# Two of eight experts for every token, the other six only for their picked tokens

## What is computed

```python
h = tok(x, ...)          # 64 images: patches -> windows (attention over 9 positions) -> 4 patch tokens and a class token, 256 wide
h = concat([cls_tok, h], axis=1)                       # 6 tokens per image, 384 rows in all
h = h + attn(layernorm(h), Wq, Wk, Wv, Wp, bp)         # 16 heads, causal, 6 tokens
h = h + ffn(layernorm(h), gate_w, gate_up_w, down_w)
...
def ffn(x, gate_w, gate_up_w, down_w):                 # 8 experts, 256 -> 2*512 -> 256
    router_probs = softmax(x @ gate_w)
    top_k_probs, top_k_idx = top_k(router_probs, 2)
    top_k_probs = top_k_probs / sum(top_k_probs)
    hidden = silu(x @ gate) * (x @ up)                 # for each expert
    expert_out = hidden @ down
    return sum over the two picked experts of expert_out * its probability
```

## Time and profile before

| | us |
|---|---|
| median of 3 runs | 228.7 (227.08 to 228.98) |
| the profiled execution's time | 228.78 |
| its span, first to last instruction | 227.0 |
| router's logits finished, on the trace's clock | 129.62 |
| experts on PE, from then to the last matmul | 129.62 to 223.5 |

### The profile page before, as it was taken

The page is one execution under the profiler, slowest core; times in us unless marked ns, Lnnn a source line. Parts: engine busy times, 40 slices in busy tenths (PEclk is TensorE's granted clock), DMA queues, the critical chain, the costliest instruction groups (busy, mean ns, idle before and its releaser), DMA issues.

```text
span 227.0 us, 4002 instructions
## 1 busy us (share of the span) xinstructions
PE 207.6 (91%) x1368; PEld 192.4 (85%) x1368; DVE 155.6 (69%) x363; ACT 101.6 (45%) x225; POOL 79.5 (35%) x91
## 2 busy tenths in 40 slices
PE   2999989999999988789587989999999999999983
PEld 2898969898987878477386889999999999999983
DVE  2565981929696767577987599576957785858541
ACT  3754581835354516334122177383718371717030
POOL 0037093555428302270643315233423332333200
PEclk9999999999999999969889999999999999999999
DMA  6999910002910000000000005172533253400004
GB/s 222 360 394 373 339 52 3 3 0 54 423 80 1 3 0 0 0 3 0 1 0 0 3 0 206 76 277 53 225 128 149 43 234 97 180 0 3 0 0 69
DMA packets 4890, 23.01 MB, mean 101 GB/s; under 512 B 694, under 2 KB 2444, under 8 KB 3724
## 3 DMA queue, kind: packets, MB, share of 16 engines
q1 hardware_dynamic: 3960, 21.26, 26.3%
q10 hardware_dynamic: 916, 1.58, 2.0%
HBM read 22.44 MB, written 0.39 MB: 101 GB/s over the span
## 4 chain that ended last, share of the span: by engine, by line
PE 82%; DVE 8%; ACT 3%; DMA 2%; issue 2%; POOL 0%; SPq 0%; DVEq 0%
PE bank L744 26%; PE bank L757 15%; PE bank L419 11%; PE bank L496 9%; PE bank L539 4%; PE bank L434 3%; DMA raw<-conv_w 2%; PE bank L443 2%; PE bank L634 2%; PE bank L618 2%; PE bank L643 1%; PE bank L476 1%; DVE stats L1162 1%; PE bank L657 1%; PE bank L694 1%
## 5 line engine op out<-in xcount | busy, mean ns | idle before, releaser
L744 PE MATMUL bank<-split 128*128 128x322 f32 x384 | 59.2, 314 | 0.6 <-DVE vprod L1531 0.6
L744 PEld LDWEIGHTS bank<-split 128*128 128x128 f32 x384 | 57.6, 188 | 0.9 <-issue 0.9
L1147 POOL TENSOR_TENSOR split<-raw,split 128x256 fp32r<-128x256 f32 x32 | 29.0, 906 | 56.7 <-DVE split L1484 56.7
L757 PE MATMUL bank<-split 128*128 128x256 f32 x288 | 36.0, 283 | 0.6 <-DVE split L1537 0.6
L757 PEld LDWEIGHTS bank<-split 128*128 128x128 f32 x288 | 35.4, 192 | 0.8 <-DVE split L1537 0.8
L419 PE MATMUL bank<-split 128*128 128x256 f32 (+1 forms) x225 | 28.2, 284 | 1.0 <-DVE split L1259 1.0
L419 PEld LDWEIGHTS bank<-split 128*128 128x128 f32 (+1 forms) x225 | 27.5, 191 | 1.5 <-DVE split L1259 1.4
L1044 POOL TENSOR_TENSOR rstd<-veps,mhalf 128x1 f32<-128x1 f32 (+2 forms) x17 | 14.2, 838 | 38.5 <-DVE veps L1169 38.4
L496 PE MATMUL bank<-split 128*128 128x512 f32 x108 | 26.9, 399 | 0.0
L1011 ACT ACTIVATE vprod<-bank 128x322 f32<-128x322 f32 x32 | 13.9, 436 | 24.8 <-PE bank L744 24.7
L1531 DVE TENSOR_TENSOR vprod<-bank,vprod 128x322 f32<-128x322 f32 x32 | 15.7, 491 | 12.0 <-PE bank L744 8.5
(11 more groups left out here) (161 smaller groups left out, 276.2 us busy)
## 6 DMA issues: line engine op xcount, KB each, us to landing
raw<-ffn_w SPq DMA_DIRECT2D x8, 1536.0 KB, 6.5
raw<-xa SPq DMA_DIRECT2D x5, 768.0 KB
tok<-tok_w SPq DMA_DIRECT2D x1, 1536.0 KB, 12.4
tok<-tok_w SPq DMA_DIRECT2D x1, 776.0 KB, 6.4
raw<-xa ACTq DMA_DIRECT2D x1, 576.0 KB, 5.1
raw<-xb SPq DMA_DIRECT2D x6, 96.0 KB
att<-att_w SPq DMA_DIRECT2D x1, 488.0 KB, 13.9
raw<-conv_w SPq DMA_DIRECT2D x1, 384.0 KB, 5.7
```

Of the source, the lines that this page charges most:

```text
L744: mm = pe.matmul(bank[b][:, 0:NCOL], aws[:, q, pw, a:a + P], ms[:, px, c, FIRST:ROWS], start=(c == 0 and m == 0), stop=(c == CC - 1 and m ...
L757: mm = pe.matmul(bank[b][:, 0:C], hids[:, px, s * FQ + q, a:a + P], bws[:, s, pw, q * C:(q + 1) * C], start=(q == 0 and m == 0), stop=(q = ...
L1147: pool.tensor_tensor(bws[:, s, LO, q * C:(q + 1) * C], b_raw[:, s, q, :], bws[:, s, HI, q * C:(q + 1) * C].bitcast(F32), ALU.subtract).the ...
```

## The change

Experts 0 and 1 (DENSE = 2) still run over all tokens. For experts 2 to 7 each token's up to two picks are given a slot: slots are sorted by expert, each expert begins at a tile of 128 slots, and there are always SLOT_TILES = 10 tiles. DVE computes the slots from the router's logits and a count of picks on PE (`count_picks`). POOL scatters the normalised rows, with token number and weight behind them (258 floats), to `expert_rows` in DRAM by six indirect DMAs, after SP has zeroed it early in the kernel. SP reads the expert of each tile from `tile_expert`, loads the tile's gate and up weights (1 MB, `tile_a`) and down weights (512 KB, `tile_b`), each into one of three slots, and its rows (132 KB, `tile_rows`). PE turns the rows, computes gate and up with the rows stationary (12 matmuls with 512 columns), turns the hidden tile (4 transposes), computes the output in plain float32 (4 matmuls) and adds it to its tokens by a matrix of zeros and ones (`give_back`, 6 matmuls). That matrix is made by POOL (`way_back`).

Between the last keys and the router: the first tile's window sum is made by DVE and POOL instead of PE, the second's in part; biases and residuals are added by matmuls into an open bank; the class attention works from unnormalised rows with centred weights; the ninth position's scores are computed on their own; DVE now makes all of `attention_products`; the tokens' blocks are taken in the order 0, 2, 1; and ACT takes over copies and normalising. The diff, cut:

```diff
+            def tile_a(s, expert):
+                if s == 1:
+                    sp.wait_ge(a_split, FQ)
+                if s == 2:
+                    sp.wait_ge(a_split, FQ + 2)
+                    sp.wait_ge(a_split_dve, 2)
+                if s >= RING:
+                    sp.wait_ge(tile_a_split, FQ * (s - RING + 1))
+                sp.dma_start(a_ring[ring(s)]...).then_inc(tile_a_in[s % RING], 16)
+            def tile_b(s, expert):
+                if s:
+                    sp.wait_ge(*((b_split, FQ * s) if s <= DENSE else (tile_down, s - RING + 1)))
+                sp.dma_start(b_ring[ring(s)]...).then_inc(tile_b_in[s % RING], 16)
+            def tile_rows(s):
+                if s >= RING:
+                    sp.wait_ge(back_done, s - RING + 1)
+                    sp.wait_ge(tile_out_split, s - RING + 1)
+                sp.dma_start(xr[:, s % RING, :], expert_rows[s * P:(s + 1) * P, :]).then_inc(rows_in[s % RING], 16)
+            sp.wait_ge(route_step, ROUTED)
+            expert = [sp.value_load(tile_expert[0:1, s:s + 1], ...) for s in range(RING)]
+            tile_a(0, expert[0])
+            tile_b(0, expert[0])
+            tile_a(1, expert[1])
+            tile_a(2, expert[2])
+            tile_b(1, expert[1])
+            expert += [...]
+            sp.wait_ge(scattered, PICKS * RT * 16)
+            for s in range(RING):
+                tile_rows(s)
+            tile_a(3, expert[3])
+            tile_b(2, expert[2])
+            tile_a(4, expert[4])
+            for s in range(3, SLOT_TILES):
+                if s + 2 < SLOT_TILES:
+                    tile_a(s + 2, expert[s + 2])
+                tile_b(s, expert[s])
+                tile_rows(s)
...
+            keys_values_group(0)
+            class_values_mean()
...
+            class_query()
             keys_values(GT * 4 + 1)
             keys_values(GT * 4 + 2)
+            class_keys()
+            keys_values_group(5)
...
+            turn_context(0, 3)
+            out_proj(0, [(3, "ctx0")])
+            turn_context(2, 1)
+            out_proj(2, [(3, "ctx0"), (1, "ctx2")])
+            turn_context(1, 4)
+            out_proj(1, [(4, "ctx1")])
+            turn_mid(0, 3)
+            turn_mid(2, 1)
+            router(0, 3)
+            router(2, 1)
+            turn_mid(1, 4)
+            router(1, 4).then_inc(filled[2], 1)
...
+            def rows_turn(s):
+                wait_tile_in(pe, rows_in, s)
+                pe.wait_ge(*((rows_split, s) if s else (route_step, PLACED)))
+                for c in range(CC):
+                    mm = pe.transpose(bank[3][:, c * P:(c + 1) * P], xr[:, s % RING, c * P:(c + 1) * P], ident)
+                mm.then_inc(rows_turned, 1)
+            gate_up(0, 0)
+            count_picks()
+            for n in range(1, FQ + 2):
+                gate_up(n % FQ, n)
+            for i, (j, b) in enumerate(OUT_BANKS):
+                down(0, j, b)
+            gate_up(2, FQ + 2)
+            gate_up(3, FQ + 3)
+            rows_turn(0)
+            for s in range(SLOT_TILES):
+                tile_gate_up(s)
+                if s + 1 < SLOT_TILES:
+                    rows_turn(s + 1)
+                if s:
+                    tile_out(s - 1)
+                if s > 1:
+                    give_back(s - 2)
+                if s + 1 == SLOT_TILES:
+                    late_down(2)
+                hidden_turn(s)
+            give_back(SLOT_TILES - 2)
+            late_down(0)
+            tile_out(SLOT_TILES - 1)
+            late_down(1)
+            give_back(SLOT_TILES - 1)
...
+            for s in range(SLOT_TILES):
+                if s:
+                    hidden_copy(s - 1)
+                if s + 1 < SLOT_TILES:
+                    tile_weights_hi(s + 1, 0)
+                tile_silu_gate(s)
+                if s + 1 < SLOT_TILES:
+                    tile_weights_hi(s + 1, 1)
+                    rows_hi_copy(s + 1)
+                    tile_weights_hi(s + 1, 2)
+                    tile_weights_hi(s + 1, 3)
+                if s == 0:
+                    for q in range(FQ):
+                        down_hi(1, q)
+                if s:
+                    out_hi(s - 1)
...
+            for q in range(FQ):
+                down_lo(0, q)
+            weights_lo(1, 0)
+            weights_lo(1, 1)
+            pool.wait_ge(route_step, WEIGHED)
+            for j in range(RT):
+                for i in range(PICKS):
+                    scatter(i, j)
+            way_back(0)
...
+            for s in range(SLOT_TILES):
+                if s + 1 < SLOT_TILES:
+                    tile_weights_lo(s + 1, 0)
+                tile_product(s)
+                if s + 1 < SLOT_TILES:
+                    rows_lo(s + 1)
+                    for piece in range(1, FQ):
+                        tile_weights_lo(s + 1, piece)
+                if s:
+                    out_lo(s - 1)
```

More of the change, by code:

```diff
@@ L105 @@
[L105 to L109, removed]
+    [f"conv{i}" for i in range(TILES) if CONV_BANK[i] == 0] + ["redT1", "q1", "agg0", "agg1", "qkv0"],
@@ L979, in _ @@
[L979 to L987 removed]
+            local_copy(0)
@@ L988, in _ @@
+            act.wait_ge(gexp_done, 1)
+            for wt in range(2):
+                k = LNS.index(f"pool{wt}")
+                ins = act.activation(gexr[:, wt, :], gexp[:, wt, :], ACT.Identity, scale=rstd[:, k, 0:1])
+            ins.then_inc(gexp_done, 1)
+            h_copy(1)
+            in_normalise(1)
+            h_copy(2)
+            hT_copy(1)
             qkv_copy("qkv0")
-            hT_copy(1)
-            wait_full(act, 4, "gvT")
-            act.copy(gvT[:, :, :].rearrange("p c n -> p (c n)"), bank[4][:, :]).then_inc(drained[4], 1)
+            copy_pair(2, "in2", hT[:, T - 1, :, :, :].rearrange("p c s b -> p c (s b)"))
@@ L1156, in _ @@
+            pool.wait_ge(rows_ready, RT + 1)
+            pool.wait_ge(route_step, WEIGHED)
+            for j in range(RT):
+                for i in range(PICKS):
+                    scatter(i, j)
+            way_back(0)
+            for q in range(FQ):
+                down_lo(1, q)
+            for s in range(1, SLOT_TILES):
+                way_back(s)
         @block.vector
@@ L1540, in expert_pair @@
-            def expert_pair(pair, last):
-                for s in range(2):
-                    e = 2 * pair + s
-                    for q in range(2, FQ):
-                        chunk(e, s, q, pair, last)
-                    if not (last and s == 1):
-                        for q in range(2):
-                            chunk(e + 1, 1 - s, q, pair + s, last)
-                    accumulate(e)
-            chunk(0, 0, 0, 0, False)
-            chunk(0, 0, 1, 0, False)
-            with dve.Fori(0, E // 2 - 1) as pair:
-                expert_pair(pair, False)
@@ new lines, in _ @@
+            hidden(3)
+            weights_lo(2)
+            for n in range(FQ):
+                hidden_lo(n)
+            weights_lo(3)
+            hidden(FQ)
+            hidden(FQ + 1)
+            hidden_lo(FQ)
+            hidden_lo(FQ + 1)
+            for i, (j, b) in enumerate(OUT_BANKS):
+                accumulate(0, j, b)
+            tile_weights_lo(0, 0)
+            tile_weights_lo(0, 1)
+            hidden(FQ + 2)
+            tile_weights_lo(0, 2)
+            hidden_lo(FQ + 2)
```

1196 lines of the change are left out of this document (782 added, 414 removed).

## The result

| | before | after |
|---|---|---|
| median of 6 runs, us | 227.89 (226.19 to 229.47) | 260.15 (255.57 to 262.65) |
| the profiled execution's time and span, us | 228.78, 227.0 | 259.73, 257.8 |
| mean granted clock of its PE | 0.985 | 0.925 |
| last keys finished on PE | 78.67 | 85.37 |
| router's logits finished | 129.61 | 131.18 |

The ratio of comparable runs is 1.130 (95% interval 1.114 to 1.145): slower by an eighth. It is lower than the ratio of the medians, since it leaves out disturbed runs, four of the six of after and the profiled one among them.

The account below looks back on a forecast made before the run. PE bounds the kernel before, and the row-load wait the new loop: logits 124.4 + 24 + 86.9 = 235.3, last addition 0.5 and stores 3.7 give 239.5, span 238.8, forecast 240.5 us; own range 232 to 247, wider 227 to 251.

Parts of the forecast that it names:

- last keys end: Start to last keys on PE: added passes and DVE work make them end at 81.0, 2.3 us later.
- last keys to R: Last keys to router's logits: reordered stages, then DVE as the bound, put the logits at 124.4, 5.2 us earlier.
- R to the first slot tile L: Router's logits to first slot-tile gate and up pass: dense work, scatters, rows and pieces take 24 us (22 to 32).
- L to the last matmul: Slot-tile loop: 86.9 us, with periods of 9.9 for tiles 3 to 7 and 6.2 for tiles 8 and 9.
- last matmul to the end: End of kernel: last addition 0.5 us, then stores as before, 3.7 us.
- The new order pays: Behind the second sum, between last keys and router: from 89.5, where it was 89.80, logits come 5.2 us earlier.
- My bound of a POOL instruction (1.64): Scatter issue on POOL: at most 1.64 us each, so six are over 17.5 us after the router's logits.
- rival 2: Scatters beside full queues land like 10.6 us; loop starts 32 us after the logits, time 249; chance 0.12.
- The price of 21 us for the wait: Slot-tile loop: waiting for rows behind weights costs 21 us, 86.9 against 65.9 without it.
- Rival 1: Loop: small row loads pass the bulk, landing about 2.9 us later; period 6.6, time 223; chance 0.15.
- transfers from SP are served in order: Loop: rows issued behind 1536 KB of weights land only after them, 6.3 + 0.3 us, making the period 9.9.
- rival 3: Loop: idle gaps halve PE's clock; a tile takes 7.4 us, hidden under 9.9, or 11.8 and time 260; chance 0.04.

Follow-up runs that it names:

- the stages run alone: Changed kernel's stages between last keys and router, all eight experts dense as before, no store of zeros, tables or slots: 224.68 us, again 224.36, against the kernel before.
- the late zeros: Changed kernel with the store of zeros started after the last patches' load instead of after the fourth: 254.65 us, ratio 1.116 to the kernel before.
- the fastest order: Changed kernel with zeros stored later, ten row buffers, fewer weights beside scatters, unused matmuls, row loads spread among weights: 223.92 us, ratio 0.985 to before.

## Why the prediction was right or wrong

The direction and the place of the loop's cost were right; the time was 240.5 (227 to 251) and came out at 260.15, outside the range. Two steps failed above all: the store of zeros, put at nothing, which cost about 5 us, and the landing of the scatters, put at 2.9 to 3.4 us beside 4.2 MB of loads, which took 7.1. On the trace's clock:

| step | predicted | measured | added |
|---|---|---|---|
| last keys end | 81.0 | 85.37 | +4.4 |
| last keys to R | 43.4 | 45.8 | +2.4 |
| R to the first slot tile L | 24 (22 to 32) | 29.0 | +5.0 |
| L to the last matmul | 86.9 | 91.7 | +4.8 |
| last matmul to the end | 4.2 | 6.6 | +2.4 |
| sum, less the 0.7 at which the clock starts: span | 238.8 | 257.8 | +19.0 |

**Up to the last keys: a term was missing.** The 2.3 us for the new values and keys lie between two measurements: 2.7 where the stages run alone, with 1.5 us of it a slow stretch at 15 to 22 us, and 1.0 with the late zeros. The store of zeros had no term at all. The change names it, and I costed it at nothing without saying what hides it. It stands in SP's list ahead of two groups of patches, and moving it behind them gave back between 4 and 5.7 us, where 4.4 were missing. The question to have asked was that of every DMA issue: which queue is it moved into, and what is behind it. Rows 6 already showed 488 KB landing 13.9 us after their issue in that same stretch: the DMA engines had no room there.

**Last keys to router: right in kind, 2.4 us short.** DVE's last block was to begin 21.2 us behind the last keys and take 10.0; its first product began at 108.14 (22.8 behind) and its last ended at 118.98 (10.8). From there to R the prediction's 12.2 us were measured as 12.2. Why the block began 1.6 us later stays open. "The new order pays" holds: 45.8 us here and 44.7 in the stages alone, against 50.9 before.

**R to the first slot tile: a landing mis-sized.** The last issue was to be over at R + 17.5; it was at R + 17.7. That was luck in part: the first scatter starts at R + 9.1 and not at R + 7.7, and the six take 8.6 us and not 9.8. My bound of a POOL instruction (1.64) held: each issue keeps POOL 0.96 to 1.51 us, and they follow each other every 1.5 us. So the 18.6 us of the estimate under rival 2 were not seen. The step that failed is "their landing is 2.9 us with free queues, or 10.6; I take 2.9 to 3.4". I had myself put 4.2 MB in flight beside them, landing until R + 21.6, and took the price of free queues. Measured: 7.1 us beside 4.2 MB, 4.8 beside 1.5, 2.7 with nothing, between my two ends. These count from the start of the issue, so by its end 6.1 us were left where I had 3: 3.3 of the 5.0 us. Of rival 2 this is a good half: it had the loop at R + 32. The other 1.7 us are the load of the rows (3.5 for 2.9) and the pieces behind it, which ran with PE at half clock.

**The loop: period right, cause too narrow.** Predicted 9.9 for tiles 3 to 7 with the rows landing about 5 us after their issue. Measured: 11.8 for tile 3, with 7.05 us to land, and then 10.1, 9.9, 9.9 and 9.8, with 4.9 to 5.5. The price of 21 us for the wait (20.6 by the prediction's own terms, which add up to 66.3 without it and not 65.9) was confirmed by the run with the rows first (21.2 less). Rival 1 is dead in the form in which it stood: rows issued behind the bulk do not pass it. But "transfers from SP are served in order" is too narrow. From ACT's queue, issued at the same point, it is as slow, so a queue of its own bought nothing. The tile's work on PE was right too: 5.87 measured for 5.9.

What the prediction had wrong inside the period is the split. It said PE would be idle for 4 us in each; the rows show 2.1 (and 6.5 ahead of tile 3). The other 1.9 us are PE running slower behind the wait (3.30 for 1.89 us at L1022, 1.52 for 1.06 at L1034 in the rows above). That is rival 3, hidden in the waiting tiles, as its text said. The slow passes stand on the chain, since the rows' buffer waits for them, but the period does not follow them: in these four periods the rows are issued 1.0 to 1.6 us behind the first weights (204.60 and 206.02 above) and land 6.5 to 6.6 us behind them every time, near the 6.6 of the prediction.

The 4.8 us lie at the two ends, in three terms. First, the clock: the first tile's 12 passes take 4.96 us instead of 3.0, and the second transposes come at L + 4.8 instead of L + 2.8; 1.4 us of it is given back by luck, as the next step takes 4.5 us where I had a whole tile's 5.9. Second, the bulk ahead of tile 3's rows, 1.9 us: I priced it as 1.5 MB, but there are 3.1 MB, the loads that stand ahead of SP's loop and those of its first step. SP's timeline:

```profile
171.22 0.34 SPq L509 DMA_DIRECT2D raw<-ffn_w  x1
171.75 1.86 SPq L503 DMA_DIRECT2D raw<-ffn_w  x2
173.80 0.33 SPq L509 DMA_DIRECT2D kv_rows<-ffn_w  x1
174.23 0.37 SPq L516 DMA_DIRECT2D window<-expert_rows  x1
```

Third, the tail: from the eighth to the tenth row transposes it is 14.4 us instead of 12.4. The eighth step is 7.5 us with no wait for rows at its end, and its output passes behind the last long wait are slow (PE's timeline: 2.55 us at L1022 and 1.84 at L1034, granted clock 0.60 and 0.54 from 222 to 226): the clock again. The ninth is 6.9 us, with 0.9 of waiting for the rows behind `tile_b`. The windows of after show the first long wait inside the loop and the fall behind it:

```profile
174.00:176.00 2.00, 0.82 (x4) 0.35 (x2) 0.88 (x2) 0.58 (x2) 0.00 (x0) 1.00 1.05 440
176.00:178.00 2.00, 0.00 (x0) 0.00 (x0) 0.00 (x0) 0.00 (x0) 0.00 (x0) 1.00 1.02 430
178.00:180.00 2.00, 0.00 (x0) 0.00 (x0) 0.00 (x0) 0.00 (x0) 0.00 (x0) 0.51 0.97 406
182.00:184.00 2.00, 2.00 (x7) 1.55 (x6) 1.54 (x3) 1.41 (x3) 0.00 (x0) 0.50 0.00 0
```

PE is idle from 175 on, the granted clock is 0.51 in the window from 178, half of 2.4 GHz, and stays there while PE is busy again. The Trainium skill, "TensorE: Matmul & The Clock Gate", section "HAM oscillation — how this bites in real kernels", describes this for waits on DMA in every tile; the trace agrees, with 0.50 to 0.54 behind each wait for rows of 2.1 to 6.9 us, and 1.00 throughout where eight unused matmuls filled one; behind the wait of 0.9 us at the tenth transposes it stays at 1.00.

**The end.** I took the 3.7 us of before for the stores. In before the last additions are 1.4 us apart, as `down` ends tile by tile: its DVE and SP timelines have, for the first of these three additions and the store behind it,

```profile
220.74 0.48 DVE L1523 SCALAR_TENSOR_TENSOR pe_rows<-bank,wgt,pe_rows 128x256 f32<-128x256 f32 x1 [0.78 <-PE bank L757]
221.25 0.62 SPq L402 DMA_DIRECT2D out<-pe_rows  x1
```

In after no tile is complete before the last `give_back`, so the three additions fall within 1.07 us and the stores are issued one behind another after them, with SP's last one at 253.34. That last issue also holds SP for 2.00 us, where in before it takes 0.48. It is 6.6 us from the last matmul to the end instead of 4.2: the last issue starts 1.5 us after the last matmul and not 0.5, and takes 1.5 us longer. The timeline of after:

```profile
251.59 1.07 DVE L2126 TENSOR_TENSOR pe_rows<-pe_rows,bank 128x256 f32<-128x256 f32 x3
252.36 3.00 ACTq L431 DMA_DIRECT2D out<-pe_rows  x3
253.34 2.00 SPq L431 DMA_DIRECT2D out<-pe_rows  x1
```

This was not tested by an experiment. That the additions come together and the last issue takes longer is in the rows; that the one causes the other is argued. The end is 4.2 us in the kernel of the stages alone, and 6.6 or 6.7 with slots in the fastest order too.

**The range.** It reached up to rival 2's 249 and counted each rival as happening alone. A half of rival 2, a part of rival 3, a missing term and an end 2.4 us longer came together, and all were on the same side.

## What to carry to other kernels

When a small load gates the next step, issue it before the bulk that it doesn't need, or a step ahead of its use; moving it to another queue at the same point did nothing here. Price every transfer that a change adds by what is in flight where it stands, and look for what is queued behind it, also where it seems to have nothing to do with the critical work. A gather that saves 10 of 92 us of matmuls needs its scatter, load and first tile hidden, or it gives all of it back: here 8 of the 10 went into getting started and 2 into the end.

## What the runs showed of the hardware

- An indirect scatter of 128 rows of 1032 bytes keeps POOL for 0.96 to 1.51 us, and six of them follow each other every 1.5 us. The last of them lands 2.7, 4.8 or 7.1 us after the start of its issue with loads of 0, 1.5 or 4.2 MB beside it.
- A load of 129 KB lands 2.0 to 2.1 us after its issue when it is issued ahead of 1.5 MB, about 5 us after it when behind, from SP's queue or ACT's alike, and 7.05 us after it behind 3.1 MB.
- A store of 1290 KB issued among the first loads took 20.0 us to land and 11.1 us behind them, and a patch load's issue that came next held SP for 7.57 us instead of 0.33.
- A matrix product of 12 passes of 512 columns took 3.0 us at a granted clock of 1.00, and 4.96 and 5.17 us, nearly all at 0.50, behind waits of 6.9 and 3.3 us; with 3.7 us of unused matmuls in the wait it took 3.06.
- The granted clock fell to 0.50 behind waits of 2.1 to 2.3 us too (tiles 4 to 6 of after), with PE busy without a gap in the 3 us ahead of each.
